# A tile's way from x to keys begun a step sooner in a fused attention and feed-forward kernel

## The reference, cut to what matters

```
xn = layernorm(x)
c_Q, c_KV, k_pe = rms_norm(xn @ Wq_down), rms_norm(xn @ Wkv_down), rms_norm(xn @ Wk_pe)
scores = q . k * SCALE, causal;  attn = softmax(scores)
out = x + (attn @ v) @ Wo + ternary(xn) @ w_rram
```

## Time and profile before

| | |
|---|---|
| median of three runs | 1884.58 us (1882.13 to 1886.13) |
| the profiled execution | 1885.12 us, its span 1883.3 us |
| PE busy | 1742.0 us, 92% of the span |
| DVE, ACT, POOL busy | 1291.6, 1135.7, 417.7 us |
| mean granted clock of PE | 0.967 of full |
| SP's DMA queue | 237.40 MB, 69.0% of 16 engines' span |

### The profile page before, as it was taken

How to read it: one execution, slowest core, us unless ns; L and a number is a source line. 1 busy time by engine, 2 the same in 40 slices (tenths; PEclk the granted TensorE clock), 3 DMA queues, 4 the chain that set the end, 5 groups by cost and what they waited for, 6 DMA issues and landing times.

```text
span 1883.3 us, 29874 instructions
## 1 busy us (share of the span) xinstructions
PE 1742.0 (92%) x9192; PEld 906.7 (48%) x9192; DVE 1291.6 (69%) x3359; ACT 1135.7 (60%) x2467; POOL 417.7 (22%) x1037
## 2 busy tenths in 40 slices
PE   3568999989999999998999999998999999999998
PEld 2325445545544445554544444554445444555543
DVE  4456777767767677775857767776767767777764
ACT  5556666656656566664656656664656656666553
POOL 0112222222221222222122222212222222221110
PEclk8779999999999999998999999999999999999999
DMA  9115677785769767785877867887786877877786
GB/s 292 26 37 102 119 142 150 149 141 105 151 114 166 144 135 140 137 150 100 153 138 145 148 115 138 156 148 123 136 145 111 154 139 142 150 142 135 144 148 110
DMA packets 917487, 255.15 MB, mean 135 GB/s; under 512 B 903120, under 2 KB 905424, under 8 KB 916944
## 3 DMA queue, kind: packets, MB, share of 16 engines
q1 hardware_dynamic: 907872, 237.40, 69.0%
q10 hardware_dynamic: 9456, 15.83, 2.9%
HBM read 20.35 MB, written 8.39 MB: 15 GB/s over the span
## 4 chain that ended last, share of the span: by engine, by line
PE 62%; issue 12%; DVE 9%; SPq 6%; DMA 5%; ACT 3%; POOL 2%; ACTq 0%; DVEq 0%; POOLq 0%
PE bank L476 5%; PE bank L480 5%; PE bank L478 5%; PE bank L479 5%; PE bank L477 5%; PE bank L499 5%; PE bank L500 4%; PE bank L501 4%; DMA FT<-F 4%; PE bank L512 4%; PE bank L513 4%; PE bank L514 4%; DVE F L1163 2%; DVE P L1150 1%; SPq L1429 1%
## 5 line engine op out<-in xcount | busy, mean ns | idle before, releaser
L781 ACT ACTIVATE P<-P,nm 128x512 f32<-128x512 f32 (+7 forms) x512 | 395.5, 773 | 616.1 <-DVE nm L1150 614.8
L1150 DVE CUSTOM_DVE_ANT_0 P<-bank,mask,neg 128x512 f32<-128x512 f32 (+7 forms) x512 | 417.1, 815 | 331.6 <-PE bank L480 328.0
L1163 DVE SCALAR_TENSOR_TENSOR F<-P,rc,F 128x512 f16<-128x512 f32 (+7 forms) x512 | 421.3, 823 | 9.6 <-ACT F L776 8.8
L776 ACT ACTIVATE F<-P,rc 128x512 f16<-128x512 f32 (+7 forms) x512 | 390.1, 762 | 45.9 <-DMA FT<-F 32.1
L499 PE MATMUL bank<-FT,V 128*128 128x512 f16 x576 | 223.8, 389 | 53.3 <-DMA FT<-F 49.4
L1316 POOL TENSOR_SCALAR sn<-sm 128x1 f32<-128x1 f32 x512 | 138.4, 271 | 575.9 <-ACT P L781 573.2
L476 PE MATMUL bank<-K,Q 128*128 128x512 f16 (+3 forms) x768 | 251.6, 328 | 10.7 <-DMA Q<-QS 7.4
L480 PE MATMUL bank<-K,Q 128*128 128x512 f16 (+3 forms) x768 | 251.7, 328 | 0.0
L479 PE MATMUL bank<-K,Q 128*128 128x512 f16 (+3 forms) x768 | 251.7, 328 | 0.0
L478 PE MATMUL bank<-K,Q 128*128 128x512 f16 (+3 forms) x768 | 251.6, 328 | 0.0
L477 PE MATMUL bank<-K,Q 128*128 128x512 f16 (+3 forms) x768 | 251.6, 328 | 0.0
(11 more groups left out here) (178 smaller groups left out, 2622.8 us busy)
## 6 DMA issues: line engine op xcount, KB each, us to landing
FT<-F SPq DMA_TRANSPOSE x512, 3.7
out<-X ACTq DMA_DIRECT2D x32, 256.0 KB, 2.8
X<-in_x ACTq DMA_DIRECT2D x28, 256.0 KB, 3.0
wo<-in_Wo SPq DMA_DIRECT2D x4, 1024.0 KB, 15.4
V<-CC SPq DMA_DIRECT2D x32, 64.0 KB, 2.1
Q<-QS SPq DMA_TRANSPOSE x128, 3.9
X<-in_x SPq DMA_DIRECT2D x4, 256.0 KB, 12.5
fw<-in_weight SPq DMA_DIRECT2D x1, 1024.0 KB, 8.3
```

The costliest lines, as they stand in the source:

```text
L776: return e.eng.activation(dst, src, ACT.Copy, scale=scale)
L781: e.eng.activation(m.P[:, u % 4, 0:w], m.P[:, u % 4, 0:w], ACT.Exp, bias=m.nm[:, u % 8:u % 8 + 1], scale=-1.0, accum_out=m.sm[:, u % 8:u % ...
L1150: e.eng.tensor_tensor_reduce(out=m.P[:, u % 4, 0:w], in0=m.pS[u % 2][:, off:off + w], in1=m.mask[:, 1024 - w:1024], scale=m.neg[:, :], sca ...
L1163: e.eng.scalar_tensor_tensor(out=m.F[:, u % FSLOTS, w:2 * w], in0=m.P[:, u % 4, 0:w], scalar=m.rc[:, u % 8:u % 8 + 1], in1=m.F[:, u % FSLO ...
```

## The change

All pieces of a tile's way from x to its turned copy are moved to earlier quarters: `stats` from (0,3) to (0,0), `ln_root` from (1,0) to (0,1), `ln` from (1,1) to (0,2), `norm` from (1,2) to (0,3), `x_hi` and `x_lo` from (1,3) to (1,0), `x_signs` from (2,0) to (1,0), `turn_x` from (2,1) to (1,2). `keys` goes from (1,2) to (1,1) and `keep` from (2,0) to (1,3). The store of the last tile's output goes from (2,2) to (1,3), the load of a new x from (3,3) to (2,3). The ring gets more candidate places for tiles with i of up to 4.

```diff
-        x = min((0, RING - k, k) if 3 * k <= RING else (0, RING - k), key=last)
+        x = min((0, RING - k, *(range(0, RING - k + 1, k) if 3 * k <= RING else ())), key=last)
...
-                if (g, q) == (1, 0):
+                if (g, q) == (0, 1):
                     tiles.ln_root(t + LEAD)
-                elif (g, q) == (1, 2):
+                elif (g, q) == (0, 3):
                     tiles.norm(t + LEAD)
-                elif (g, q) == (1, 3):
+                elif (g, q) == (1, 0):
                     tiles.x_hi(t + LEAD)
...
-            if (g, q) == (2, 2) and t:
+            if (g, q) == (1, 3) and t:
                 store_out(t - 1)
-            if (g, q) == (3, 3) and t + LEAD + 1 < T:
+            if (g, q) == (2, 3) and t + LEAD + 1 < T:
                 load_x(t + LEAD + 1)
...
-                if (g, q) == (0, 3):
+                if (g, q) == (0, 0):
                     tiles.stats(t + LEAD)
-                elif (g, q) == (1, 1):
+                elif (g, q) == (0, 2):
                     tiles.ln(t + LEAD)
-                elif (g, q) == (2, 0):
+                elif (g, q) == (1, 0):
                     tiles.x_signs(t + LEAD)
...
-            if (g, q) == (1, 3) and t + LEAD < T:
-                tiles.x_lo(t + LEAD)
             if t and t + LEAD - 1 < T:
                 if (g, q) == (1, 0):
                     tiles.rotate_keys(t + LEAD - 1)
-                elif (g, q) == (1, 2):
+                elif (g, q) == (1, 1):
                     tiles.keys(t + LEAD - 1)
+            if (g, q) == (1, 0) and t + LEAD < T:
+                tiles.x_lo(t + LEAD)
...
-            if (g, q) == (2, 1) and t + LEAD < T:
+            if (g, q) == (1, 2) and t + LEAD < T:
                 tiles.turn_x(t + LEAD)
-            if (g, q) == (2, 0) and t and t + LEAD - 1 < T:
+            if (g, q) == (1, 3) and t and t + LEAD - 1 < T:
                 tiles.keep(t + LEAD - 1)
```

## The result

The changed kernel takes 1928.54 us (median of four runs, 1923.29 to 1932.73), the kernel before 1883.66 in the same runs: a ratio of 1.0236 (95% interval 1.0206 to 1.0266). It is 45 us slower, where 6.6 us of gain were forecast and the range ended at 1892.

A forecast was written before the change was run, and what follows sets the result against it. It took PE's 49.4 us of waits for transposed probabilities, mostly at (3,0) with `keep` ahead of h3, as the bound. Waits -14.3, `up` +7.1, clock -3.4, load +4.0 gave -6.6: 1884.6 to 1878.0 us, range 1862 to 1892.

The forecast's parts named there:

- What bounds the kernel, and the place: PE's 49.4 us of waits for transposed probabilities, mostly at `weigh` of (3,0), where `keep` holds h3 up.
- XT ahead of h1: SP's queue, tile 5: h3 0.6 us earlier despite XT, 1.4 more if h1's issue shrinks; -0.9 us per tile taken.
- The term for FT and Q, -14.3: PE's waits for transposed probabilities and Q, mostly at (3,0), fall by 14.3 us in sum, bounds 0 and -30.
- Rival B: Transfers decide: nine large tiles lose 1.0 us each, +15 us against the forecast's average; 1895 us (1890 to 1898), chance 0.20.
- The store at nothing: The output store, three quarters sooner, falls into the same busy stretch as before and costs nothing.
- the load at 4.0: `load_x` at (2,3), beside V and h3, costs 0.3 us in each of 13 tiles: +4.0 us, bounds 0 and +12.
- `up` behind `x_signs`, +7.1: DVE's `x_signs` ahead of `rotate` delays `up` at (1,2), 1.1 us in six tiles: +7.1 us, bounds +2 and +12.
- The clock, -3.4: PE's low clock eases where tiles 13 and 21's long wait splits, 1.7 us each: -3.4 us, bounds -14 and +5.
- At nothing: Earlier `ln`, `norm`, `x_hi`, `ln_root`, `stats`, `keys`, the ring's new places and the earlier store were priced at zero.
- The ring: The ring's new candidate places cost nothing; where the user was three steps back nothing had waited.
- ACT's pieces: Earlier pieces on ACT cost nothing, since DVE and ACT have idle time in step 0.
- That `keep` early fills idle time of SP: `keep` (3.8 us) and XT fill the time SP waited for probabilities between h0, h1 and h2.

The follow-up runs named there:

- e13: Kernel before with only `keep` moved from (2,0) to (2,1), behind h3 and XT: 1847.7 us.
- e5: Changed kernel with only XT (`turn_x`) back at (2,1), `keep` staying at (1,3): 1887.0 us.
- e11: Changed kernel with XT back at (2,1), store and load back at (2,2) and (3,3), `keep` staying early: 1876.2 us.
- e2: Changed kernel with only the output store and the load of x back at (2,2) and (3,3): 1899.8 us.
- e10: Kernel before with only the store moved to (1,3) and the load to (2,3): 1912.4 us.
- e8: Changed kernel with only the load of x back at (3,3), the store staying at (1,3): 1912.4 us.
- e3: Changed kernel with only POOL's `x_lo` a quarter later, at (1,1): 1921.9 us.
- e9: Changed kernel with store and load back, `keep` at (2,1) behind h3, XT at (1,1) ahead of h0, `x_signs` at (1,1) behind `rotate`: 1818.5 us.
- e14: Changed kernel with XT, `keep`, store and load all back, leaving the earlier ACT, DVE and POOL pieces and the ring: 1896.6 us.
- e4: Changed kernel with only XT and `keep` back at (2,1) and (2,0), store and load staying early: 1893.7 us.

## Why the prediction was wrong, point by point

**What bounds the kernel, and the place.** Right: the waits stood at (3,0), `keep` ahead of h3 made most of them, and `turn_x` behind it did not (e13: `keep`'s line alone takes the waits for FT from 49.4 to 19.5 us and the time down by 36.9). It was also right that Q would get behind both and PE would wait twice, and that `up` at (1,2) would pay.

**XT ahead of h1, the step that failed first.** The term was "+1.5 (XT) - 2.1 = 0.6 us earlier; if h1's issue, 2.28 us, shrinks to the usual 1.4". It took XT as 1.5 us of SP's time that idle time swallows, and let h1's issue get shorter or stay. The runs show that it gets longer: h1 now stands 0.09 us behind XT, and takes 2.22 us in tile 10 (1.23 before) and 2.21 in the median of tiles 1 to 28 (1.33 before; 1.33 again with XT back, e5). Standing close behind a transpose is not enough for that: before, in tile 10, Q is issued 0.18 us behind h2 and takes 1.43. What it is in the queue that makes h1 slow behind XT is not shown. Nor were the 2.28 us of tile 5 a matter of closeness. In tiles 13 and 21, which have the same i and nearly the same gap ahead of h1 (0.99 and 1.00 us; 0.86 in tile 5), it took 1.43 and 1.42; in tile 5 the slices of 7 to 9 GB/s fall into it. The 3.15 us of the changed kernel hold such a stretch too, and tiles 13 and 21 have 2.59 and 2.17.

The term for FT and Q, -14.3 with 4.0 for the load, came out at +21.2 (53.4 to 74.6). By PE's timelines the waits at (3,0) went from 34.7 to 50.0 us in the nine tiles with i of 5 to 7, where the forecast took 5.7 off, and from 7.2 to 8.5 in the four with i = 2, where it took 5.6 off. XT's move alone is 41.5 us in the change (e5) and 23.6 without the early store and load (e11 against e2).

Rival B was right in the direction and too small. It had the sign: in tile 9 h3 lands 21.2 us after h0's issue, where it was 18.5, and in the nine large tiles 1.8 us later on average. But it named 1.0 us in each of them, and left the small tiles their gain; tile 10 had none (1.89 us). Its time, 1895, is over 30 us short.

**The store at nothing, the load at 4.0.** "The store of the output, sooner by three quarters, falls into the same busy stretch as before" is the second step that failed. Store and load cost 28.5 us alone in the old order (e10) and 28.7 in the change (e2), the load 16.1 of them (e8). The load had the right sign, and its bound of 12 was near; but the 0.3 us a tile was a guess: in tile 10 of e10, with the load issued from ACT 0.12 us behind it, h3 lands 3.8 us after its issue and not 2.8. That 214 GB/s is the most that the engines move of transposes was a wrong reading of the earlier trace rows: they hold three slices of 283 to 289, from 408.6 to 409.95 us, in which all 1,536 packets are of SP's queue and of 256 bytes, and SP had issued only transposes (the last at 406.47).

**`up` behind `x_signs`, +7.1.** Right cause, wrong size: +13.3. I priced `x_signs` as it ran alone (1.07 us) and did not ask what POOL does in the same quarter; with `x_lo` beside it, it takes 2.01. The overlap is shown by e3, which removes 11.8 us of waits. In tile 6 of the change the first instruction of `x_signs`, begun 0.09 us after POOL's subtraction, ended 0.29 us after it and took 1.37 us in place of 0.42. What of POOL's work holds DVE up is not shown.

**The clock, -3.4.** The low clock was to get less, and PE's busy time came out at +11.0. That a split wait gives 1.7 us back was my estimate from the 6.7 us at 0.50 of the earlier trace rows; no run shows it. What the runs show is more waits and a lower clock together: the waits for Q and FT are 35 in place of 23, and 74.6 us in place of 53.4, at a mean clock of 0.958 in place of 0.967; in e9 they are 18.7 us at 0.981, and PE is busy 1717.5 us in place of 1742.0.

**At nothing.** The ring: right (1.0005). ACT's pieces: nothing to be seen beside `up` in e14. That `keep` early fills idle time of SP was right where XT is late: there it gains 20.4 us (e14 to e11).

**Left open.** Store and load early cost 28 us in the old order with the pieces late (e10 to before), but nothing in the old order with the pieces early: e4 has them and e14 does not, and their intervals overlap. The traces hold a likely reason. In tile 10 of e4 the load goes out at 689.23, 0.95 us ahead of h3, in e10 0.12 us behind it. In the nine large tiles it goes out 1.5 to 2.2 us ahead of h3 in e4 and h3 lands 4.2 us after its issue, as in the kernel before; in e10 it goes out 0.7 to 1.4 us ahead and h3 lands 4.8 us after (means of nine). No run moved the load alone in the old order to try it. So no sum of single costs gives the 45 us exactly.

## What to carry to other kernels

When a transfer is moved in a queue, count what stands between it and the deadline of everything behind it. Do not price it at its own issue alone: here what was issued directly behind XT got longer (h1's issue, 1.33 to 2.21 us in the median) and so did what landed beside store and load (h3 3.4 to 4.5 us in e10), and by how much was to be had only from a run. Look for the place where the queue waits anyway (here ahead of h0, for the ring, 1.1 to 3.0 us in tiles with i of 5 and more), and for what has the latest deadline (`keep`, needed only in the next tile): the kernel with that order, and with `x_signs` behind `rotate`, is 66 us faster than before, where the change was 45 slower. For each piece moved on one engine, look up what the other engines run in that quarter: here `rotate` started 1.07 us after `x_signs` before, and 2.01 us after it in tile 6 of the change, with POOL's `x_lo` beside it.

## What the hardware showed that I had not expected

The second DVE instruction of `x_signs` (L909) takes 1.52 us (median of 32) in the change, where POOL's subtraction runs beside `x_signs`, and 0.69 in all 32 tiles of e3, where it doesn't.

In tile 10 of e10 the load of x (256 KB, from ACT) is issued 0.12 us after h3 (701.61 and 701.49), and h3 lands 3.8 us after its issue; in the kernel before, without the load there, it lands 2.8 us after. Over tiles 1 to 28 the median is 4.5 us in e10 and 3.4 before.

In tile 5 of both kernels the DMA engines have a short stretch in which few packets begin. Here is the changed kernel from 411 to 420 us in 40 slices of 0.225 us, with five slices of 9 to 27 GB/s from 415.0 on, then 257 to 291. Both rows count a packet in the slice in which it begins, so the digit 0 does not say that the engines are free: 19 packets of 256 bytes that began between 414.4 and 415.0 us took 1.3 to 1.8 us each, up to 416.2.

```profile
DMA  0499999999999879990000099999999992089800
GB/s 3 88 215 207 214 209 224 207 183 188 333 411 353 146 162 198 118 50 9 9 27 17 19 257 291 289 286 279 291 288 290 291 291 42 3 171 221 179 10 0
```

In the kernel before show 7 and 9 GB/s from 407.25 to 408.15, after 18 packets of 256 bytes that began from 407.1 to 407.2 and took 1.4 us each. In both kernels a packet of 16 KB of queue q8, which the profile calls an instruction queue, had begun 0.5 us ahead of the first of the long packets, at 413.92 us (it took 0.93) and at 406.61 (1.11); whether that is the cause was not tried.
